# A state scan fed by TensorE: its input rows are packed on 72 partitions instead of 96

## The reference, cut to what matters

```
def step(h, inputs):                       # h: (batch, 16 states, 512 channels), fp32
    ad, bd, xt, ct = inputs                # decay, B row, normalised x row, C row of one token
    h = jnp.clip(h * ad[:, :, None] + bd[:, :, None] * xt[:, None, :], -10.0, 10.0)
    yt = jnp.einsum('bd,bdh->bh', ct, h)
    return (h, yt)
```

## Time and profile before

| | us |
|---|---|
| median of 3 runs | 1749.14 |
| the profiled execution's own time | 1756.73 |
| its span, first to last instruction | 1754.9 |
| TensorE busy (matmul) | 1624.7 |
| VectorE busy | 1559.3 |
| ScalarE busy | 1213.4 |
| GpSimd busy | 584.8 |

### The profile page before, as it was taken

How to read it: one execution, slowest core, us unless ns; L and a number is a source line. 1 busy time by engine, 2 the same in 40 slices (tenths; PEclk the granted TensorE clock), 3 DMA queues, 4 the chain that set the end, 5 groups by cost and what they waited for, 6 DMA issues and landing times. The chain is left out here.

```text
span 1754.9 us, 42114 instructions
## 1 busy us (share of the span) xinstructions
PE 1624.7 (93%) x14036; PEld 707.1 (40%) x14036; DVE 1559.3 (89%) x2132; ACT 1213.4 (69%) x2017; POOL 584.8 (33%) x821
## 2 busy tenths in 40 slices
PE   7999999999999999889999889999997899998898
PEld 3555555555554554422222114544553222221144
DVE  5899999999987999899999888769999999998965
ACT  5555656556555999889989873069997899888800
POOL 0223224223231112246555542002213465555500
PEclk9999999999999999899999999999998999999999
DMA  4000001200001356566868897723465767798877
GB/s 165 1 1 1 1 2 60 79 2 0 1 2 37 139 173 179 186 209 181 235 199 233 226 237 209 255 84 129 151 205 190 209 195 225 200 248 214 223 222 268
DMA packets 121314, 253.27 MB, mean 144 GB/s; under 512 B 50832, under 2 KB 76688, under 8 KB 101136
## 3 DMA queue, kind: packets, MB, share of 16 engines
q1 hardware_dynamic: 120768, 249.92, 47.7%
q10 hardware_dynamic: 432, 1.84, 0.3%
HBM read 164.54 MB, written 87.16 MB: 143 GB/s over the span
## 5 line engine op out<-in xcount | busy, mean ns | idle before, releaser
L2069 DVE CUSTOM_DVE_ANT_0 q<-R,PS 128x768 f32<-128x768 f32 x756 | 595.2, 859 | 31.2 <-PE PS L1524 23.4
L1068 ACT ACTIVATE R<-q,Ast 128x512 f32<-128x512 f32 x756 | 510.4, 715 | 83.3 <-DVE q L2069 35.5
L635 POOL TENSOR_TENSOR R<-q,Ast 128x256 f32<-128x256 f32 x504 | 308.6, 612 | 294.7 <-DVE q L2069 250.8
L1524 PE MATMUL PS<-xq,Uw 96*128 96x512 bf16 (+1 forms) x1280 | 338.0, 348 | 55.1 <-DMA xq<-xpart_d 16.3
L1537 PE MATMUL PS<-q,Wy 128*32 128x512 f32 x2048 | 280.9, 613 | 3.8 <-ACT ys L1057 2.9
L1524 PEld LDWEIGHTS PS<-xq,Uw 96*128 96x128 bf16 x1280 | 87.1, 98 | 429.3 <-DVE q L2069 362.4
L1189 PE MATMUL PS<-X,Win 128*128 (+1 forms) x456 | 213.8, 606 | 0.1
L1090 PE MATMUL PS<-xn,Wl 128*128 128x512 f32 x384 | 187.9, 614 | 0.7 <-DVE xn L1651 0.7
L1769 DVE SCALAR_TENSOR_TENSOR acc<-xp,Wc,acc 128x512 f32<-128x512 f32 x192 | 134.5, 749 | 2.6
L567 POOL TENSOR_TENSOR ex<-ex,rs 128x1024 f32<-128x1024 f32 x32 | 76.8, 2400 | 164.3 <-DVE rs L1674 164.3
L1189 PEld LDWEIGHTS PS<-X,Win 128*128 128x128 f32 x456 | 82.6, 191 | 92.5 <-issue 91.7
(11 more groups left out here) (159 smaller groups left out, 2475.3 us busy)
## 6 DMA issues: line engine op xcount, KB each, us to landing
xq<-xpart_d SPq DMA_DIRECT2D x384, 192.0 KB
Uw<-bdiag_d SPq DMA_DIRECT2D x96, 256.0 KB, 6.0
sg_d<-sg SPq DMA_DIRECT2D x16, 1024.0 KB, 5.4
xn_d<-z SPq DMA_DIRECT2D x16, 1024.0 KB, 4.0
y_d<-ys SPq DMA_DIRECT2D x64, 256.0 KB, 5.2
xnp<-xn_d SPq DMA_DIRECT2D x12, 1024.0 KB, 10.5
sgp<-sg_d SPq DMA_DIRECT2D x12, 1024.0 KB, 14.3
xpart_d<-xh SPq DMA_DIRECT2D x16, 512.0 KB, 3.0
```

The source lines that it names most:

```text
L635: pl.tensor_tensor(R[:, 1, cols], q[:, (t + 1) % 2, 1, cols], Ast[:, h, 1, t:t + 1].broadcast_to([P, DI // 2]), ALU.mult).then_inc(pd_r, 1)
L1068: act.activation(R[:, w, :], q[:, (t + 1) % 2, w, :], ACT.Copy, scale=Ast[:, h, w, t:t + 1]).then_inc(ac_r, 1)
L1524: pe.matmul(PS[:, bank, begin:end], Uw[0:XROWS, u, s8 % 8, w, :, :].rearrange("p b n -> p (b n)"), xq[0:XROWS, hb, s8 % XT, w, begin:end], ...
L2069: v._custom_dve(bass.dve_ops.TENSOR_ADD_SAT, out=state, in0=R[:, :, :].rearrange("p w c -> p (w c)")[:, begin:end], in1=fed, s0=CLIP, s1=- ...
```

## The change

The step SPREAD becomes PARTS = 3. Row (j, b) of x now lies on partitions 3 (8 j + b) + i, so 72 partitions in a row without zero rows, and the contraction has 72 rows instead of 96. `Uw` and `bdiag_d` follow (DIAG = 3 x S x ROW). `load_b` has 3 DMAs of 24 rows of 8 KB (192 KB) instead of 32 rows (256 KB). `load_x` has the same bytes as before, on every third partition. The zeroing of `bdiag_d` takes 6 DMAs for each pass instead of 8. `still_d`, its two stores, the two loads of it in each layer and TensorE's waits for them are gone.

```diff
-SPREAD = 4
+SPREAD = PARTS
 XROWS = SPREAD * PARTS * GB
...
-DIAG = 4 * S * ROW
+DIAG = PARTS * S * ROW
...
-    still_d = scratch("still_d", (PARTS * GB, XB // 2 * QW * XT * DI), bf16)
...
-        one_in = [sem("still_rows0"), sem("still_rows1")]
...
-            still = still_d.rearrange("r c -> (r c)").rearrange("(k p c) -> p k c", p=P, k=2)
-            for k in range(2):
-                sp.dma_start(still[:, k, :], words(zeros).bitcast(bf16)[:, 0:PARTS * GB * XB * QW * XT * DI // (4 * P)]).then_inc(zero_in, 16)
...
-                def still_rows(b):
-                    half_x = xq[:, b * (XB // 2):(b + 1) * (XB // 2), :, :, :].rearrange("p k g t c -> p (k g t c)")
-                    for i in range(PARTS, SPREAD):
-                        sp.dma_start(half_x[i:XROWS:SPREAD, :], still_d).then_inc(one_in[b], 16)
...
-                    sp.wait_ge(zero_in, 16 * PASSES * (GB * DIAG // (P * 1024)) + 32)
+                    sp.wait_ge(zero_in, 16 * PASSES * (GB * DIAG // (P * 1024)))
...
-                still_rows(0)
...
-                still_rows(1)
...
-                    if first and s8 in (0, 4):
-                        pe.wait_ge(one_in[s8 // 4], (l + 1) * (16 * (SPREAD - PARTS)))
```

More of the change, by code:

```diff
@@ L1510, in _, with inputs @@
                 alone(pe)
-                def inputs(pi, k, s8, c=None, first=False):
+                def inputs(pi, k, s8, c=None):
                     c2 = k if c is None else c * 2 + k
@@ L1539, in y_of @@
                         mm.then_inc(pe_yq, 1)
-                inputs(l * PASSES, 0, 0, None, True)
+                inputs(l * PASSES, 0, 0)
                 for ps in range(PASSES):
@@ L1548, in _ @@
                                 last_group(c2 * 8 + s8)
-                            inputs(pi, c2, s8 + 1, None, ps == 0 and c2 == 0)
+                            inputs(pi, c2, s8 + 1)
                             y_of(pi, c2, s8)
```

## The result

The changed kernel took 1781.37 us (median of 4 runs, 1774.88 to 1789.39) beside 1749.24 us for the kernel before (4 runs, 1744.36 to 1760.18): a ratio of 1.0179, 95% interval 1.0137 to 1.0221. That is 32 us more where I forecast 7 us less. A later measurement gave 1.0164 [1.0132, 1.0195]. The profiled execution took 1789.4 us (span 1787.6), at the top of those runs; its granted clock, 0.951, was the lowest of the four (the others had 0.962 to 0.964), so it shows more of the clock's part than a typical run.

The account below looks back on a forecast made before the run. VectorE was taken to bound the scan, with DMA backlog causing its waits. B loads gave -7.4 us and all other terms 0, so 1749.1 became 1741.7 us; the range for 8 in 10 was 1732 to 1757.

Parts of the forecast that it names:

- What bounds the kernel: In the scan, VectorE's three pieces set each step; fewer or faster loads can give back at most 19.2 us.
- B loads: Loads ahead of two late waits in each layer: each shrinks from 3.71 to 2.78 us, in all -7.4 us.
- The first rival: B loads: 12 engines are kept as long as 16 were, so no change, 1749 us; chance 0.28.
- x loads: 26 loads ahead of the waits, same bytes on every third partition: +13.0 to -11.2 us, taken as 0.
- the placement rival: Rows below partition 64 bound the loads: x loads slow, B loads save nothing, +13.0 us, 1762 us; chance 0.13.
- the line I had drawn: Placement decides from 0.28 us for an x load, below 230 GB/s, if B loads give their 7.4.
- Matmul with 72 rows: Input matmuls in the scan: 87 ns each either way, covered by 362.4 us of waits, 0; costlier-matmul rival 0.02.
- SP's issue: SP issuing 24-row loads: +0.9 us for each load_b if row count is the reason; taken as 0, upper bound 3.6 us.
- Zero rows of xq: Two 384 KB loads a layer vanish before the scan: 0, at most -3 us if the first x load were late.
- the forecast's signs: In the scans: VectorE idle 21.3 to some 14 us, x loads alone near 258 GB/s, calm windows 19.8 of 20.
- placement's signs: In the scans: x loads alone near 212 GB/s and longer waits; that rival's chance 0.13.
- the matmul's: Signs of a costlier matmul: line 1524 slower and VectorE idle in the calm windows; chance 0.02.

Follow-up runs that it names:

- base 28: Changed kernel with its 72 packed rows moved to partitions 28 to 99, zeros elsewhere: 1741.32 us (0.9955) with 100-row matmuls, 1741.87 us (0.9947) with 128.

## Why the prediction was wrong

*What bounds the kernel: right in part.* VectorE sets the pace while TensorE's clock is up, and backlog of the DMA engines caused the waits. But "a cheaper matmul buys nothing by itself" and "cover it" rested on the 362.4 us in which weight loads waited for VectorE. That is not TensorE's slack: these waits lie beside its own running matmuls. A step is 1.04 + 1.06 = 2.1 us of matmuls in 2.42 us, so some 0.3 us is free, not 1.4 (less than the 0.44 us that I let it cover); and at 1.2 GHz the same step is 3.7 us, so TensorE is the bound by 1.3 us.

*B loads: right in size, not in its working.* Forecast -7.4 us, measured alone -7.0 us (0.9960 [0.9941, 0.9980]). But the load is not the 2.78 us of the estimate: 590/178 = 3.3 us alone in the kernel after, 590/184 = 3.2 in the one that packs only B, against 786/225 = 3.5 before. The rate did not hold at 212; engines count (0.76 of them busy), though less than in proportion. 0.2 to 0.3 us at eight places is 2 us, not 7. In a queue shared with other transfers a load also takes 25% fewer bytes and leaves four engines free, which may be worth more than its own duration; that was argued, not measured. The first rival (no gain, engine count) falls by the time and holds in part by the rate.

*x loads: the step that failed first.* I wrote "Eight x loads ... +13.0 to -11.2 us. I take 0, the row of x loads themselves". The sign was that of the placement rival, which I had given 0.13; its upper bound was too small as well: alone the packing costs 22.6 us (1.0129), not 13.0. The price for a load was about right: 590/197 = 3.0 us or 590/208 = 2.8 instead of 590/251 = 2.35, 0.5 to 0.65 us more, or 0.4 us more by the longer measure, and the line I had drawn, 0.28 us or 230 GB/s, was crossed. What I under-counted is, by the waits, where it applies: I took 26 loads ahead of four waits, and the kernel with packed x waits in 11 places instead of 7. That the rate would be that of the row was an assumption against a rule I had quoted: the Trainium skill, "SBUF — State Buffer", section "Door 1: The DMA port swizzle (why `[64,N]` ≈ `[32,N]`)", by which all of partitions 0 to 63 share half of the ports. The runs agree with it where most rows lie below 64: 64 of 72 give 197 to 208 GB/s. Between 48 and 36 they show no order: 251, 259 and 268 GB/s in three profiles with 48, and 265 with 36.

*Matmul with 72 rows: failed.* "Nothing in the trace speaks for it, and I take 0", with a chance of 0.02. Alone it costs 13 us (1.0075). Not by a slower matmul, as that rival had it, but by TensorE's clock, which after a gap mostly stayed at 1.2 GHz for 7 to 48 us of nearly unbroken work, where with 96 rows it was back in 3. The rows that could have warned stand in the trace of before: its granted clock was 0.96 in 928 to 1056, so each wait already cost some clock, and the kernel sits 0.3 us a step from being bound by TensorE. That the row count of a matmul bears on how soon the clock returns, no row of one kernel can show.
The Trainium skill, "TensorE: Matmul & The Clock Gate", section "Part 1: The HAM clock gate (the "warmup" mystery)", tells of the clock as set by how busy TensorE has been. The trace here disagrees if busy is taken as the busy time of the profile: 3.00 of 3.00 us busy, window after window, at 0.50. With 96 rows, and the same busy time, it came back.

*SP's issue: right.* SP waited 228.7 us for TensorE at line 407 (189.8 before), and the DMAs of 24 consecutive rows cost it less than those of 32, not 726 ns (line 402 of the kernel after; shortest, median and longest ns, first and last start):

```profile
L402 SPq DMA_DIRECT2D Uw<-bdiag_d x96: 340/365/548, 683.6 to 1658.3; - x96
```

So 726 ns belongs to the strided form of the x loads, not to 24 rows. *Zero rows of xq: right.* The first input matmul starts at 741.87 us, 0.56 us earlier than at 742.43 in the profile of before, and waits for no load.

*Of the forecast's signs:* of the 20 us windows of the earlier trace rows the calm one stayed at 19.84 us, and the others had 14.47, 12.62, 18.64 and 15.80 where they had 16.25, 18.98, 18.62 and 15.06; x loads alone did not stay near 258 GB/s, and VectorE's idle in the two stretches went up to 20.02 + 18.75 = 38.8 us. Of placement's signs the slower x loads (197 GB/s) appeared, the longer waits only in the later profile and in the run with x packed alone. Of the matmul's, line 1524 read slower (374 ns instead of 348, by the clock) and VectorE idled in 988 to 1008, a window with little loss before. So two rivals held at once; I had priced each by itself and none together.

## What to carry to other kernels

Before packing rows to save bytes, count how many of the rows that a DMA writes fall on either side of partition 64, and don't let nearly all fall on one: with matmuls of 128 rows the same packed loads were 1.1% slower than the unpacked kernel at partitions 0 to 71 and 0.5% faster at 28 to 99. The runs fit a border at 64; no other border was tried against it. Rows of zeros in a matmul's contraction are not waste where TensorE has gaps and little slack: dropping from 96 to 72 rows cost 0.75% through the clock, while going to 128 changed nothing. Read TensorE's slack from the time of a step in its timeline, at both clock levels, not from the waits of its weight loads.

## What the runs showed of the hardware

- With matmuls of 72 rows TensorE's clock stayed low longer. Stretches at 1.2 GHz with TensorE busy for 95% or more lasted 3 us with 96 rows or more, and up to 34 and 48 us with 72. All stretches within the scans: 41 us before, 126 us with only the row count changed, 164 and 116 us in two profiles of the kernel after, 68 us with 96 rows and longer waits (both the packed kernel with zero rows and x packed alone), 27 and 24 us with 100 and 128 rows at base 28. By what rule the row count acts is open: only 72, 96, 100, 120 and 128 rows were run.
- Strided x loads of 24 rows ran, where little else was in flight, at 197 to 208 GB/s with 64 of 72 rows below partition 64, at 251 to 268 with 48, at 262 with 39 and at 265 with 36. B loads hardly changed with placement: 172 to 184 GB/s on partitions 0 to 71, 184 and 188 on 28 to 99.
- DMAs of 24, 32 and 40 rows kept 0.76, 1.03 and 0.63 of the engines busy. The Trainium skill, "DMA: Bandwidth & Descriptors", section "Why a DMA increments its semaphore by 16 and not by 1", has the number of engines as the largest up to 16 that divides the rows, 12, 16 and 10; the shares agree. Rates went 178, 225 and 197 GB/s, so less than in proportion to engines.
- What stays open: how the B loads' 7.0 us arise, when a load alone is only 0.2 to 0.3 us shorter, and why the whole kernel at a spread of five loses 18 us.
